# A conditioned residual with LoRA in fp32r: wider warming matmuls, another order of loads, and x tile 0 transposed by VectorE

## The reference

```python
# x (64, 32, 512) f32; ids: 64 of 0..15 and 64 of 0..2
# W0 (16, 32, 32), W (512, 512), A (5, 512, 32), Bw (512, 32)
x = x + einsum('bct,bcd->bdt', x, W0[ids0])
base  = einsum('bsi,oi->bso', x, W)
low   = einsum('bsi,bir->bsr', x, A[ids1])
delta = einsum('bsr,or->bso', low, Bw) * 0.5
return x + base + delta
```

## Time and profile before

| what | value |
|---|---|
| median of 3 runs | 88.79 us (87.93, 88.79, 89.1) |
| the profiled execution | 88.51 us |
| its span, first to last instruction | 86.7 us |
| PE busy | 82.6 us (95%), 463 matmul records |
| DVE, ACT, POOL busy | 55.8, 39.6, 23.3 us |
| DMA moved | 10.16 MB, mean 117 GB/s |

### The profile page before, as it was taken

How to read it: one execution, slowest core, us unless ns; L and a number is a source line. 1 busy time by engine, 2 the same in 40 slices (tenths; PEclk the granted TensorE clock), 3 DMA queues, 4 the chain that set the end, 5 groups by cost and what they waited for, 6 DMA issues and landing times.

```text
span 86.7 us, 1411 instructions
## 1 busy us (share of the span) xinstructions
PE 82.6 (95%) x463; PEld 72.9 (84%) x463; DVE 55.8 (64%) x117; ACT 39.6 (46%) x80; POOL 23.3 (27%) x37
## 2 busy tenths in 40 slices
PE   5999999999999999999999999999999999999950
PEld 5999999998888988898889888988898888889940
DVE  3672879975984696469744984499249933731550
ACT  0544492233547573457255616551754273415440
POOL 5322798977008001800170008000710000000000
PEclk9999999999999999999999999999999999999999
DMA  1999990370000494646037502770250015000606
GB/s 27 314 350 310 199 188 19 83 178 12 8 0 8 147 267 81 203 126 176 2 140 230 134 0 83 230 186 0 80 177 0 0 50 192 8 0 3 239 14 228
DMA packets 12393, 10.16 MB, mean 117 GB/s; under 512 B 1508, under 2 KB 9572, under 8 KB 12388
## 3 DMA queue, kind: packets, MB, share of 16 engines
q1 hardware_dynamic: 11444, 9.24, 38.1%
q10 hardware_dynamic: 432, 0.59, 2.1%
q0 software_dynamic: 512, 0.26, 1.7%
HBM read 5.90 MB, written 4.19 MB: 116 GB/s over the span
## 4 chain that ended last, share of the span: by engine, by line
PE 95%; DVE 1%; issue 0%
PE p_u L588 15%; PE p_u L589 15%; PE p_u L590 15%; PE p_low L573 5%; PE p_low L578 5%; PE p_low L574 4%; PE p_low L639 4%; PE p_u L599 4%; PE p_y L605 4%; PE p_y L606 4%; PE p_y L608 4%; PE p_u L616 3%; PE p_y L588 2%; PE p_y L589 2%; PE p_y L590 2%; PE p_y L643 2%
## 5 line engine op out<-in xcount | busy, mean ns | idle before, releaser
L252 POOL DMA_INDIRECT w_sel<-in_L_cond_weights,w_row x16 | 16.3, 1019 | 33.4 <-DVE diag L499 30.3
L588 PE MATMUL p_u<-m_hi,xt_hi 128*128 128x512 f32 (+1 forms) x60 | 22.6, 377 | 0.0
L589 PE MATMUL p_u<-m_lo,xt_hi 128*128 128x512 f32 (+1 forms) x60 | 22.6, 377 | 0.0
L590 PE MATMUL p_u<-m_hi,xt_lo 128*128 128x512 f32 (+1 forms) x60 | 22.5, 375 | 0.0
L410 DVE TENSOR_TENSOR xt_lo<-xt,xt_hi 128x512 fp32r<-128x512 f32 x14 | 10.1, 728 | 8.4 <-ACT xt_hi L308 8.4
L396 DVE STREAM_TRANSPOSE xt<-x_sb 128x512 f32<-128x512 f32 x14 | 15.1, 1091 | 0.0
L416 DVE TENSOR_TENSOR u_lo<-p_u,u_hi 128x512 fp32r<-128x512 f32 (+1 forms) x15 | 9.3, 652 | 8.9 <-ACT u_hi L313 8.8
L318 ACT ACTIVATE y_sb<-p_y 128x512 f32 (+1 forms) x13 | 7.7, 591 | 12.2 <-PE p_y L608 12.2
L590 PEld LDWEIGHTS p_u<-m_hi,xt_lo 128*128 128x128 f32 x60 | 11.3, 188 | 2.1
L588 PEld LDWEIGHTS p_u<-m_hi,xt_hi 128*128 128x128 f32 x60 | 11.3, 188 | 1.9
L589 PEld LDWEIGHTS p_u<-m_lo,xt_hi 128*128 128x128 f32 x60 | 11.3, 188 | 1.8
(11 more groups left out here) (92 smaller groups left out, 126.7 us busy)
## 6 DMA issues: line engine op xcount, KB each, us to landing
x_sb<-in_x SPq DMA_DIRECT2D x28, 128.0 KB
out<-y_sb SPq DMA_DIRECT2D x7, 512.0 KB, 3.2
w_sb<-in_L_cond_W ACTq DMA_DIRECT2D x2, 256.0 KB, 3.9
w_sb<-in_L_cond_W SPq DMA_DIRECT2D x2, 256.0 KB, 3.8
x_rows<-in_x SPq DMA_DIRECT2D x2, 256.0 KB, 4.5
out<-y_sb SPq DMA_DIRECT2D x2, 256.0 KB, 2.1
a_sb<-in_L_cond_lora_A SPq DMA_DIRECT2D x1, 256.0 KB, 5.3
w_sel<-in_L_cond_weights,w_row POOLq DMA_INDIRECT x16
```

The lines of the kernel that those rows point to most:

```text
L252: nc.gpsimd.indirect_dma_start(out=w0_sel[:, t, :], out_offset=None, in_=W0_rows, in_offset=bass.IndirectOffsetOnAxis(ap=w0_row[:, t:t + 1 ...
L588: mm(to, xt_hi[:, slot, c, rows], m_hi[:, c, cols], start=(c == 0 and half != 1), stop=False)
L589: mm(to, xt_hi[:, slot, c, rows], m_lo[:, c, cols], start=False, stop=False)
L590: mm(to, xt_lo[:, slot, c, rows], m_hi[:, c, cols], start=False, stop=False)
```

## The change

- The warming matmuls are six of 128x512 in fp32r (before: seven of 128x128 in f32).
- SP issues Bw, four quarter loads of tile 0 in the pairs' layout (into the left half of `x_sb` slot 0), W pieces 3 and 2, the rows of tile 1, A[1:5], and the loads of pair 1; before the loads of pair 2, which overwrite that slot, it waits for the transpose of tile 0.
- ACT issues A[0], W pieces 1 and 0, and then the two id vectors.
- Tile 0 is transposed by DVE (L477 of the new file) and split from SBUF by ACT and DVE.
- POOL casts the ids to `ids_r` and adds the identity to all four pieces of W, in this order.
- TensorE transposes no rows of tile 0. The rows of tile 1 are transposed ahead of the second `lora_half`.
- POOL computes `ad_lo` ahead of the first two gathers. DVE spreads the first gathered matrices (`spread(0, ...)`) after the first `keep_low` and `split_low`; ACT has `hi_kept(0)` ahead of `hi_diag(0, 0)`.

```diff
-    WARM = 7
+    WARM = 6
...
-        warm = sb("warm", [P, P])
+        warm = sb("warm", [P, P], F32R)
...
             sp.dma_start(bw_sb[:], Bw.rearrange("(o p) r -> p o r", p=P)).then_inc(s_bw_in, 16)
-            sp.dma_start(w_sb[:, 0], W[0:P, :]).then_inc(s_w_in[0], 16)
-            sp.dma_start(x_rows[:, 0], x_tile[0]).then_inc(s_rows_in[0], 16)
-            sp.dma_start(ids_i[:, 0], cond.unsqueeze(0)).then_inc(s_cond_in, 16)
-            sp.dma_start(ids_i[:, 1], label.unsqueeze(0)).then_inc(s_label_in, 16)
-            sp.dma_start(w_sb[:, 2], W[2 * P:3 * P, :]).then_inc(s_w_in[2], 16)
-            sp.dma_start(x_rows[:, 1], x_tile[1]).then_inc(s_rows_in[1], 16)
+            for q in range(Q):
+                sp.dma_start(x_sb[R * q:R * (q + 1), 0, 0], x_pair[0, q, :, 0:BT]).then_inc(s_first_in, 16)
+            for o in W_ORDER[2:]:
+                sp.dma_start(w_sb[:, o], W[P * o:P * (o + 1), :]).then_inc(s_w_in[o], 16)
+            sp.dma_start(x_rows[:], x_tile[1]).then_inc(s_rows_in, 16)
             sp.dma_start(a_sb[:, 1:NL].rearrange("p l c r -> p l (c r)"), A_cols[:, 1:NL]).then_inc(s_a_in, 16)
             load(1, 1)
+            sp.wait_ge(s_first_t, 1)
             load(2, 0)
...
-            for o in W_ORDER[2:]:
+            pool.wait_ge(s_cond_in, 16)
+            pool.wait_ge(s_label_in, 16)
+            nc.gpsimd.tensor_copy(ids_r[:], ids_i[:]).then_inc(s_ids, 1)
+
+            for o in W_ORDER:
                 pool.wait_ge(s_w_in[o], 16)
                 w_diag = w_sb[:, o, P * o:P * (o + 1)]
-                nc.gpsimd.tensor_tensor(w_diag, w_diag, ident[:], ALU.add).then_inc(s_diag_right, 1)
+                nc.gpsimd.tensor_tensor(w_diag, w_diag, ident[:], ALU.add).then_inc(s_diag, 1)
...
+            pool.wait_ge(s_adiff, 1)
+            pool.wait_ge(s_adhi, 1)
+            nc.gpsimd.tensor_tensor(ad_lo[:], a_diff[:], ad_hi[:].bitcast(F32), ALU.subtract).then_inc(s_adlo, 1)
             pool.wait_ge(s_w0_row, BT)
             gather(0)
             gather(1)
...
-            act.dma_start(w_sb[:, 1], W[P:2 * P, :]).then_inc(s_w_in[1], 16)
-            act.dma_start(w_sb[:, 3], W[3 * P:4 * P, :]).then_inc(s_w_in[3], 16)
+            for o in W_ORDER[:2]:
+                act.dma_start(w_sb[:, o], W[P * o:P * (o + 1), :]).then_inc(s_w_in[o], 16)
+            act.dma_start(ids_i[:, 0], cond.unsqueeze(0)).then_inc(s_cond_in, 16)
+            act.dma_start(ids_i[:, 1], label.unsqueeze(0)).then_inc(s_label_in, 16)
+
+            def split_first():
+
+                act.wait_ge(s_first_t, 1)
+                nc.scalar.activation(xt_hi[:, 0, :, 0:P], xt[:, 0], COPY).then_inc(s_xhi, 1)
...
+            hi_kept(0)
             hi_diag(0, 0)
-            hi_kept(0)
...
-            dve.wait_ge(s_pool, 3)
-            for o in W_ORDER[:2]:
-                dve.wait_ge(s_w_in[o], 16)
-                w_diag = w_sb[:, o, P * o:P * (o + 1)]
-                nc.vector.tensor_tensor(w_diag, w_diag, ident[:], ALU.add).then_inc(s_diag, 1)
-
+            dve.wait_ge(s_first_in, 16 * Q)
+            nc.vector.transpose(xt[:, 0].rearrange("p c (b s) -> p c b s", s=S),
+                                x_sb[:, 0, 0].rearrange("p b (i c) -> p c b i", c=C)).then_inc(s_first_t, 1)
...
-            spread(0, 0, used=1)
             dve.wait_ge(s_keep, 1)
             keep_low(0)
             split_low(0)
+            spread(0, 0, used=1)
             split_diag(0, 0)
...
-                mm(p_low[:, 0:P], warm[:], warm[:], start=True, stop=True)
+                mm(p_low[:], warm[:], warm[:].unsqueeze(1).broadcast_to([P, 4, P]), start=True, stop=True)
...
             pe.wait_ge(s_diag, 2)
             transpose_w(1)
-            transpose_rows(0, p_low)
             spread_ids()
...
-            pe.wait_ge(s_diag_right, 1)
+            pe.wait_ge(s_diag, 3)
             transpose_w(2)
-            pe.wait_ge(s_diag_right, 2)
+            pe.wait_ge(s_diag, 4)
             transpose_w(3)
+            pe.wait_ge(s_ids_sb, 1)
+            pe.wait_ge(s_rows_in, 16)
+            rows_t = x_rows[:].rearrange("p (t c) -> p c t", c=C)
+            for c in range(C):
+                last = mm(p_fold[:, P * c:P * (c + 1)], rows_t[:, c], ident[:], start=(c == 0), stop=(c == C - 1),
+                          is_transpose=True)
+            last.then_inc(s_rows_t, 1)
             lora_half(1)
-            pe.wait_ge(s_ids_sb, 1)
-            transpose_rows(1, p_fold)
```

More of the change, by code:

```diff
@@ L102, in conditioned_lora_kernel @@
         w0_sel = sb("w0_sel", [P, TILES, S])
-        x_rows = sb("x_rows", [P, 2, T])
+        x_rows = sb("x_rows", [P, T])
         x_sb = sb("x_sb", [P, 2, 2, BT, J])
@@ L132, in conditioned_lora_kernel @@
         s_w_in = [sem(f"s_w_in{i}") for i in range(OC)]
-        s_rows_in = [sem(f"s_rows_in{i}") for i in range(2)]
+        s_first_in = sem("s_first_in")
+        s_rows_in = sem("s_rows_in")
         s_x_in = [sem(f"s_x_in{i}") for i in range(2)]
@@ L148, in conditioned_lora_kernel @@
         s_diag = sem("s_diag")
-        s_diag_right = sem("s_diag_right")
+        s_first_t = sem("s_first_t")
         s_adiff = sem("s_adiff")
@@ L261, in _ @@
             cond_v = ids_all[:, 0].rearrange("p (k b) -> p b k", b=BT)
-            pool.wait_ge(s_diag_right, 2)
+            pool.wait_ge(s_diag, 4)
             for j in range(BT):
@@ L281, in _ @@
             gather(1)
-            pool.wait_ge(s_adiff, 1)
-            pool.wait_ge(s_adhi, 1)
-            nc.gpsimd.tensor_tensor(ad_lo[:], a_diff[:], ad_hi[:].bitcast(F32), ALU.subtract).then_inc(s_adlo, 1)
             for p in range(1, PAIRS):
@@ L295, in _, with split_rows @@
             act.dma_start(a_sb[:, 0].rearrange("p c r -> p (c r)"), A_cols[:, 0]).then_inc(s_a0_in, 16)
-            act.dma_start(w_sb[:, 1], W[P:2 * P, :]).then_inc(s_w_in[1], 16)
-            act.dma_start(w_sb[:, 3], W[3 * P:4 * P, :]).then_inc(s_w_in[3], 16)
[L299 to L303, removed]
+            for o in W_ORDER[:2]:
[5 more added lines that the diff above has]
+                nc.scalar.activation(xt_hi[:, 0, :, 0:P], xt[:, 0], COPY).then_inc(s_xhi, 1)
+            def split_rows():
+                act.wait_ge(s_rows_t, 1)
+                nc.scalar.activation(xt_hi[:, 0, :, P:ROWS],
+                                     p_fold[:].rearrange("p (c r) -> p c r", c=C), COPY).then_inc(s_xhi, 1)
             def split_x(t, slot, u):
@@ L329, in _ @@
             nc.scalar.activation(a_stack[:], p_y[1][:], COPY).then_inc(s_a_stack, 1)
-            split_rows(0, p_low)
+            split_first()
             split_m(0, 0)
             split_m(0, 1)
-            split_rows(1, p_fold)
+            split_rows()
             split_m(1, 0)
@@ L397, in transpose_x, with split_first, split_rows @@
                                     x_sb[:, slot, u].rearrange("p b (i c) -> p c b i", c=C)).then_inc(s_xt, 1)
[L399 to L404, removed]
+            def split_first():
+                dve.wait_ge(s_xhi, 1)
+                nc.vector.tensor_tensor(xt_lo[:, 0, :, 0:P], xt[:, 0], xt_hi[:, 0, :, 0:P].bitcast(F32),
+                                        ALU.subtract).then_inc(s_xlo, 1)
+            def split_rows():
+                dve.wait_ge(s_xhi, 2)
+                nc.vector.tensor_tensor(xt_lo[:, 0, :, P:ROWS], p_fold[:].rearrange("p (c r) -> p c r", c=C),
+                                        xt_hi[:, 0, :, P:ROWS].bitcast(F32), ALU.subtract).then_inc(s_xlo, 1)
             def split_x(t, slot, u):
@@ L431, in split_low @@
                                         ALU.subtract).then_inc(s_keptlo, 1)
-            nc.vector.memset(warm[:], 1.0).then_inc(s_warm, 1)
+            nc.vector.memset(warm[:].bitcast(F32), 1.0).then_inc(s_warm, 1)
             for j in range(BT):
@@ L444, in _ @@
                                            ALU.add).then_inc(s_row_of, 1)
-            nc.vector.tensor_copy(ones_r[:], warm[0:1, :]).then_inc(s_ids, 1)
+            nc.vector.tensor_copy(ones_r[:], warm[0:1, :].bitcast(F32)).then_inc(s_ids, 1)
             dve.wait_ge(s_bw_in, 16)
@@ L509, in _ @@
             dve.wait_ge(s_x_in[1], 16 * Q)
+            dve.wait_ge(s_xlo, 1)
             transpose_x(1, 0)
```

4 lines of the change are left out of this document (1 added, 3 removed).

## The result

| | before | changed |
|---|---|---|
| median, 4 runs each | 88.62 us (87.93 to 89.1) | 90.86 us (90.01 to 92.71) |
| ratio to before, 95% | | 1.0234 (1.0183 to 1.0286) |
| profiled execution, its span | 88.51, 86.7 us | 90.01, 87.9 us |
| time less span | 1.8 us | 2.1 us |
| first matmul of tile 0 | 10.45 us | 11.09 us |

What follows compares the result with a forecast made beforehand. TensorE was taken to bound the kernel (95% of the chain of waits). From 88.51, less 0.2 (earlier main part) and 0.65 (three stops), came 87.6 us; the forecast's own range was 87.0 to 88.2, the wider one 86.8 to 89.0.

Steps and rivals of the forecast that it cites:

- Cover for the gathers that go later: Pair 0: gathers issued by about 16.0, read by VectorE at 17.7; diagonal blocks wanted only at 25 us; no cost.
- `mix` not waiting for a gather: Sign on VectorE in pair 0: `mix` starts without a wait for the later gathers, which it reads at 17.7.
- the ids' landing: Preparation: ids land at 5.6 (bounds 4.8 to 6.6), W's transposes start at 6.55, main part at 10.25, 0.2 us earlier.
- the three stops: TensorE in pair 0, near 12, 16 and 18 us: gone through reordering, together 0.65 us.
- The rival "clock": Preparation: gaps make TensorE's clock rise late; up to 2.8 us slower, 90.4; chance 0.08.
- Tile 0 through VectorE: Preparation: VectorE's transpose and the splits, second `m_lo` done at 9.8 to 10.4, hide behind TensorE's list.
- Its list is shorter by 0.48: TensorE's list before the main part loses tile 0's transposes, 0.48 us, leaving 3.7 us from W's transposes on.
- Warming: Start of preparation: six wide matmuls take 2.9 us against 3.36; following transposes up to 0.4 us earlier, if the next item is ready.

Runs made afterwards that it cites:

- e15: Kernel before with `ad_lo` ahead of the first two gathers, and SP waiting for these gathers ahead of pair 3's loads: 91.06 us, 1.0279.
- e12: Kernel before with `ad_lo` alone moved ahead of the first two gathers: 92.46 us, 1.0429.
- e3: Changed kernel with the first two gathers ahead of `ad_lo` again and the ids' cast behind the additions to W pieces 1 and 0: 89.36 us, 1.0118.
- e2: Changed kernel with the ids' cast behind the additions to W pieces 1 and 0: 90.10 us, 1.0202.
- e7: Kernel before with VectorE's wait for the ids and their cast ahead of its two additions to W: 89.27 us, 1.0108.
- e16: Changed kernel with tile 0 as rows again: one 256 KB load, transposed by TensorE, split from PSUM: 91.82 us, 1.0319.
- e9: Kernel before with only the reorderings around pair 0 on TensorE, VectorE and ScalarE; loads, ids, additions and gathers as before: 88.13 us, 0.9975.
- e1: Changed kernel with the first two gathers ahead of `ad_lo` again, as before: 90.09 us, 1.0175.
- e4: Changed kernel with SP waiting for the first two gathers to land before it issues pair 3's loads: 90.49 us, 1.0194.
- e14: The changed kernel itself, measured again against the kernel before: 91.40 us, 1.0325.
- e5: Kernel before with the six wide fp32r warming matmuls alone, 10 runs: 88.28 us, 1.0003.
- e6: Changed kernel with four more wide warming matmuls filling TensorE's gap ahead of W's transposes: 90.29 us, 1.0231.
- e8: Changed kernel with the ids' cast behind two additions to W, and `spread(0)` behind the second `split_low` on VectorE: 90.14 us, 1.0145.
- e17: Changed kernel with ids' cast behind two W additions, gathers ahead of `ad_lo`, half of pair 0's last half tile ahead of the `ad_lo` matmuls: 89.33 us, 1.0119.
- e11: Kernel before with tile 0 alone changed: four quarter loads, transposed by VectorE, split from SBUF: 89.66 us, 1.0145.
- e13: Kernel before with the reorderings around pair 0 and half of pair 0's last half tile ahead of the `ad_lo` matmuls, 8 runs: 87.87 us, 0.9937.

## Why the prediction was wrong, step by step

- **The failed step: "Cover for the gathers that go later".** It had the second gather issued by 16.0, 1.3 us later than before (14.74), read by VectorE at 17.7, and priced this at nothing. It was issued by 17.59, 2.85 later than before, and used at 20.22, so the sign "`mix` not waiting for a gather" failed. Three errors. First, `ad_lo` ended at 14.99 and not at 13.6: 0.7 because GpSimd's chain starts later by what the ids' wait and the loads cost (`a_diff` ended at 12.87 instead of 12.14), and 0.65 because the sum took the gathers' 2.4 us off `ad_lo`'s old end and forgot that ScalarE's `ad_hi`, 12.18 to 12.82 before, had run under them. Second, a gather that comes late shares the engines with pair 3's loads (e15 against e12). Third, of what stands behind it on VectorE it named `keep_low(1)`, but neither named nor priced the 7.38 us from there to pair 2's last split. That chain had half a microsecond of slack in the kernel before; it ended at 27.47, and TensorE wanted it at 28.05. Cost 1.22 us; shown by e3 (`mix` early, chain 7.37 us, no stop). That late gathers alone stop TensorE is shown by e12, there by way of `keep_low(0)`.
- **Mis-sized: the ids' landing.** 5.6 assumed, 6.4 measured (the cast's start), inside the bounds (4.8 to 6.6). The rest of that step held in sum: 10.25 plus 0.8 is 11.05, measured 11.09. Within it two small errors cancel: cast and addition took 0.77 instead of 0.95, TensorE's list 3.92 instead of 3.7. e2 and e7 show the wait in both directions, 1.0 us each. The rule of the Trainium skill on queues taking turns ("DMA: Bandwidth & Descriptors", section "Queues, rings and completion order"), by which I estimated 5.3, gave a time 1 us too early; its direction has something for it: with large pieces on the other queue (e16, one profile) they came 1.4 later still.
- **Right: the three stops**, 0.65 predicted and 0.64 found. But they were no gain to keep: e9 shows that a stop removed ahead of a fixed end only moves behind it.
- **The rival "clock" was given 0.08, and the median lies 0.85 us above the best execution.** A late or lost clock is seen directly in profiles of e1, e4 and e14, kernels with the gap, and cost 1.2 to 2.5 us in the start of the main part, against the 2.8 priced. For the changed kernel's other executions there is no profile; two of them, with spans of 89.2 and 89.7, had a mean clock of 0.981. The Trainium skill's sentence ("TensorE: Matmul & The Clock Gate", section "What's actually happening"), that the throttled state is the default and activity lifts it, agrees with these profiles. That the gap ahead of W is the cause is only supported, by e5, e6 and e7 together (no gap, gap filled, gap put in), on few executions each; e8 had a late clock without it. So the gap is a likely cause, not the only one.
- **Tile 0 through VectorE hid, but its loads did not.** In both profiles of the changed kernel TensorE goes from its list into the main part without waiting for VectorE, as forecast (in e3 and e17, where it is earlier, it starts some 0.1 us late). "Its list is shorter by 0.48" was true and worth nothing (e11: start at 10.44), since W's last pieces and with them GpSimd's chain came later: 1.2 us slower in the median. That the four issues or small pieces on SP delay them is the likely reason; no run takes them apart.
- **Warming**: no effect, as counted (e5).
- **Sums.** The forecast's terms give 87.66, not 87.6, and 256 KB at 355 GB/s take 0.74 us, not 0.72; neither matters.
- **Open:** what makes the 0.3 us outside the span. The time less the span is 2.0 to 2.25 in all forms of the changed kernel, 1.75 to 1.95 in all of the old one, except e11 with two of four at 2.2. Also open is why the landing of W's pieces scatters by over 1 us.

The forecast's sum, with what was measured: 87.6 + 0.8 (ids) + 1.2 (gathers) + 0.3 (outside) = 89.9, the best execution (90.01); the median is 0.9 higher, which a late clock can explain.

## What to carry to other kernels

Before a tiny load or a gather is put ahead of, or behind, other work on an engine, write down that engine's whole chain to the next thing that the bound engine wants, with its slack: half a microsecond of slack is no cover for three of delay. When an instruction is moved ahead of others, look for what it waits for: the work that used to cover that wait may be what you moved it ahead of. The tiny id loads here landed no earlier than the big ones ahead of them, so don't let big work wait for such loads. An added gap can cost more than its length where the bound engine's clock depends on its work. And a stop is worth removing only with the one that stands behind it: the reorderings of e9 gave 0.2 to 0.3 us, not clear of noise, and with that of e13 0.5.

## What the runs showed of the hardware

- A stop of 2.8 us in the middle of dense work was followed, 1.5 us after the work went on, by 3.3 us at a granted clock of 0.51 (e12). In e1, 1.8 us after a gap of 1.33 us, it was at 0.52 for 3.5 us.
- The clock row shows the fall from the upper level, but in these profiles it shows 1.00 where the upper level has not yet come (before, 4 to 5 us; e14, 7 to 9 us); there the distance between matmuls is the sign (0.214 against 0.12 us a transpose).
- Six fp32r warming matmuls of 512 columns (2.9 us) gave the same time as seven f32 ones of 128 (3.36 us): 1.0003 (0.9976 to 1.0029).
- 512 bytes of ids, asked for at 2.7 us behind two 256 KB pieces on their queue, had landed by 6.2 to 6.4 us, and by 7.8 with larger pieces on the other queue (e16, one profile).
- GpSimd's additions of 128x128, one behind the other, took 0.43 each, and its cast of 1x128 took 0.28. VectorE's same cast took 0.21 to 0.47, in five of nine profiles 0.21.
